# Attention row maxima: turned on TensorE and copied by two engines, or turned on VectorE and carried by DMA

## The reference

```
x = x + conv(ln(x)); t = x + ffn(ln(x))          # x: 4 images x 1024 tokens x 192
q, k, v = heads(x @ W + b)                       # 12 heads of 16
attn = q k^T / 4 + bias_h + bias_w               # 1024 x 1024 for each image and head
out  = softmax(attn) @ v ; conv = out @ Wp + bp
```

## Time and profile before

| | before |
|---|---|
| median of three runs | 905.75 us |
| profiled execution, its own time | 904.3 us |
| its span in the profile | 902.5 us |
| PE busy | 791.0 us, 88% of the span |
| DVE busy | 743.8 us, 82% |
| ACT busy | 558.8 us, 62% |
| POOL busy | 423.4 us, 47% |

### The profile page before, as it was taken

How to read it: one execution, slowest core, us unless ns; L and a number is a source line. 1 busy time by engine, 2 the same in 40 slices (tenths; PEclk the granted TensorE clock), 3 DMA queues, 4 the chain that set the end, 5 groups by cost and what they waited for, 6 DMA issues and landing times. The chain is left out here.

```text
span 902.5 us, 15297 instructions
## 1 busy us (share of the span) xinstructions
PE 791.0 (88%) x5848; PEld 407.7 (45%) x5848; DVE 743.8 (82%) x1493; ACT 558.8 (62%) x609; POOL 423.4 (47%) x263
## 2 busy tenths in 40 slices
PE   5899554479999999999999999999999999678874
PEld 2555454134444444444444444444444442256653
DVE  6998855498989988988998999998888894069995
ACT  1333345027777777777777777777777778447773
POOL 3777794436364454637263735445373324112220
PEclk9999788589999999999999999999999999889986
DMA  7676599999439392948567493939395000433411
GB/s 193 212 226 206 164 300 374 256 194 208 90 88 188 77 200 60 205 85 190 111 147 154 109 191 74 198 68 201 63 206 96 13 12 12 134 105 123 140 36 53
DMA packets 65675, 130.06 MB, mean 144 GB/s; under 512 B 9465, under 2 KB 45306, under 8 KB 57146
## 3 DMA queue, kind: packets, MB, share of 16 engines
q1 hardware_dynamic: 57634, 115.95, 56.2%
q10 hardware_dynamic: 7968, 13.13, 4.2%
HBM read 89.73 MB, written 34.60 MB: 138 GB/s over the span
## 5 line engine op out<-in xcount | busy, mean ns | idle before, releaser
L1065 DVE TENSOR_REDUCE at_piece_neg<-at_r_ps 128x1 f32<-128x512 f32 x768 | 482.8, 682 | 68.1 <-PE at_r_ps L935 64.7
L1028 ACT ACTIVATE at_probs<-at_s_ps 128x1024 f32<-128x1024 f32 x384 | 371.9, 1021 | 130.6 <-PE at_s_ps L956 129.3
L935 PE MATMUL at_r_ps<-op_mix_k,op_mix_q 128*128 128x256 f16 (+1 forms) x1920 | 282.0, 257 | 29.9 <-DMA op_mix_q<-bias_parts 17.8
L935 PEld LDWEIGHTS at_r_ps<-op_mix_k,op_mix_q 128*128 128x128 f16 x1920 | 148.2, 98 | 295.1 <-DVE at_piece_neg L1065 194.1
L850 POOL COPY op_mix_q<-op_mix_q 2x4096 f16<-2x4096 f16 x48 | 172.6, 3596 | 231.0 <-ACT op_mix_q L1033 230.5
L956 PE MATMUL at_s_ps<-op_mix_q,op_mix_k 128*128 128x512 f16 x768 | 227.7, 380 | 1.1 <-ACT at_probs L1028 0.5
L970 PE MATMUL at_o_ps<-at_probs,op_v_u 128*32 128x512 f32 x1536 | 204.2, 604 | 0.0
L218 POOL MEMSET op_mix_q<- 2x10240 f32 x12 | 103.5, 8627 | 0.6
L1033 ACT ACTIVATE op_mix_q<-at_r_ps 2x1024 f16<-2x1024 f16 x48 | 48.5, 1011 | 60.7 <-PE at_r_ps L946 60.7
L956 PEld LDWEIGHTS at_s_ps<-op_mix_q,op_mix_k 128*128 128x128 f16 x768 | 73.4, 98 | 19.6 <-ACT at_probs L1028 10.7
L854 POOL TENSOR_TENSOR at_o_sb<-at_o_sb,at_inv_rows 128x512 f32<-128x512 f32 x24 | 30.7, 1280 | 86.2 <-DVE at_inv_rows L1092 86.2
(11 more groups left out here) (121 smaller groups left out, 674.4 us busy)
## 6 DMA issues: line engine op xcount, KB each, us to landing
op_mix_q<-qk_parts SPq DMA_DIRECT2D x48, 640.0 KB, 10.7
op_mix_q<-bias_parts SPq DMA_DIRECT2D x120, 120.0 KB, 10.3
op_mix_q<-bias_parts SPq DMA_DIRECT2D x72, 128.0 KB, 10.3
bias_parts<-op_mix_q ACTq DMA_DIRECT2D x8, 1024.0 KB, 13.1
qk_parts<-op_mix_q SPq DMA_DIRECT2D x24, 256.0 KB, 2.3
v_rows<-pr_v_st SPq DMA_DIRECT2D x8, 768.0 KB, 4.1
op_mix_k<-qk_parts SPq DMA_DIRECT2D x48, 128.0 KB, 13.1
op_v_u<-v_rows SPq DMA_DIRECT2D x12, 512.0 KB, 14.2
```

The lines of the kernel that those rows point to most:

```text
L935: last = pe.matmul(r_bank("piece", at)[:, first % GROUP:first % GROUP + n], mix_q[owner.buf][:, variant, j, qt * P:(qt + 1) * P], mix_k[ow ...
L1028: act.activation(probs[n % PRING][:, 2 * pair:2 * pair + 2, :], s_ps[pair][:, :, :], ACT.Exp).then_inc(exp_done, 1)
L1065: dve.tensor_reduce(piece_neg[half][:, i:i + 1], r_bank("piece", at)[:, :], AX_X, ALU.max, negate=True).then_inc(reduced, 1)
```

## The change

Each half's 16 columns of maxima (four heads x four query tiles) are joined at once, with three operations of 16 columns in place of two times three of 8, at steps 4 and 12. DVE then turns the float16 tile of 128x32 (both parts side by side) in 32x32 blocks. ACT issues a transfer of the result to a small tensor in DRAM (128 runs of 64 bytes) at steps 5 and 13; POOL waits for it to land and issues five transfers from DRAM, one for each variant of the operand (two rows of four runs of 1 KB each). PE waits for the first of the five ahead of the first step of a half and for the other four ahead of the third. PE's transposes and the copies on ACT and POOL are gone, and with them two identity tiles and a third constant. The ring of three banks now runs on through all units. LEAD is 4, so four more pieces lie ahead of the first scores. On POOL, spread_max(unit, 1) moves from two places ahead of and behind zero_max to one ahead of it.

```diff
-    LEAD = 3
+    LEAD = 4
@@
-        for half in range(2):
-            for pair in range(2):
-                JOIN_AT[half, pair] = ((1 - half) * KT + (pair + 1) * (KT // 2) - LEAD) % STEPS
-                TURN_AT[half, pair] = JOIN_AT[half, pair] + 1
+        JOIN_AT = (2 * KT - LEAD, KT - LEAD)
+        ROWS_AT = (JOIN_AT[0] + 1, JOIN_AT[1] + 1)
@@
-        def r_bank(*use):
-            return r_ps[bank_of[use]]
+        def r_bank(unit, at):
+            return r_ps[(unit.u * PIECES + at) % RING]
@@ POOL
-                pool.tensor_copy(rows[:, 1:, :, :], rows[:, 0:1, :, :].to_broadcast([2, ops.VARIANTS - 1, 2, GROUP])).then_inc(max_spread, 1)
+                src = max_dram[half].rearrange("(h j t) p -> h j (t p)", h=2, j=QUAD)
+                pool.wait_ge(max_out[half], (unit.u + 1) * 16)
+                for variant in range(ops.VARIANTS):
+                    pool.dma_start(mix_q[unit.buf][MAX_ROW:MAX_ROW + 2, variant, :, half * GROUP:(half + 1) * GROUP],
+                                   src).then_inc((max_spread if variant else max_in)[half], 16)
@@ POOL, emit
-                spread_max(unit, 1, 0)
                 if not unit.first:
-                    pool.wait_ge(max_spread, unit.u * 4 + 3)
+                    pool.wait_ge(ops.max_zeroed, min(unit.u + 2, UNITS))
                     normalise(unit.after(-1), 1)
+                spread_max(unit, 1)
...
-                spread_max(unit, 1, 1)
-                if not unit.last:
-                    spread_max(unit.after(1), 0, 0)
...
                 normalise(unit, 0)
                 if not unit.last:
-                    pool.wait_ge(norm_done, unit.u * 2 + 1)
-                    spread_max(unit.after(1), 0, 1)
+                    spread_max(unit.after(1), 0)
@@ PE
-            def turn(unit, half, pair):
...
-                for t in range(2 * TILES):
-                    last = pe.transpose(max_rows(half * 2 + pair)[:, t * P:(t + 1) * P], neg_max[half][:, pair * 2 * TILES + t, :], ident16[:, :])
@@ PE, emit
+                    if n % KT == 0:
+                        pe.wait_ge(max_in[n // KT], (unit.u + 1) * 16)
                     if n % KT == 2:
-                        pe.wait_ge(max_spread, unit.u * 4 + (n // KT + 1) * 2)
+                        pe.wait_ge(max_spread[n // KT], (unit.u + 1) * (16 * (ops.VARIANTS - 1)))
@@ ACT
-            def row_max_in(unit, half, pair):
...
+            def max_to_rows(unit, half):
+                count = unit.u * 2 + half + 1
+                act.wait_ge(max_turned, count)
+                need(act, max_in[half], unit.u * 16)
+                need(act, max_spread[half], unit.u * (16 * (ops.VARIANTS - 1)))
+                act.dma_start(max_dram[half].rearrange("c (b r) -> b c r", r=SLOT), max_cols[half][:, :]).then_inc(max_out[half], 16)
@@ DVE, join_max
+                dve.tensor_tensor(row_neg[half][:, :], halves[:, :, 0], halves[:, :, 1], ALU.min).then_inc(row_joined, 1)
+                dve.tensor_tensor(neg_max[half][:, 0, :], halves[:, :, 0], halves[:, :, 1], ALU.min).then_inc(neg_hi, 1)
+                dve.wait_ge(row_joined, count)
                 dve.wait_ge(neg_hi, count)
+                dve.tensor_tensor(neg_max[half][:, 1, :], row_neg[half][:, :], neg_max[half][:, 0, :], ALU.subtract).then_inc(neg_done, 1)
+                dve.wait_ge(neg_done, count)
+                dve.transpose(max_cols[half][:, :], neg_max[half][:, :, :].rearrange("p h r -> p (h r)")).then_inc(max_turned, 1)
```

More of the change, by code:

```diff
@@ L792, in phase_attention @@
         BEFORE, AFTER = (0, 1, 1, 2, 2), 3
[L796 to L818, removed]
@@ L820, in phase_attention @@
-        assign(1)
-        assign(0)
-        def r_bank(*use):
-            return r_ps[bank_of[use]]
[L826 to L835, removed]
@@ L858, in _ @@
             ops.zero_max(pool, 1)
-            for pair in range(2):
-                spread_max(Unit(0, 0, 0), 0, pair)
+            spread_max(Unit(0, 0, 0), 0)
             def emit(unit):
-                spread_max(unit, 1, 0)
                 if not unit.first:
-                    pool.wait_ge(max_spread, unit.u * 4 + 3)
+                    pool.wait_ge(ops.max_zeroed, min(unit.u + 2, UNITS))
                     normalise(unit.after(-1), 1)
+                spread_max(unit, 1)
+                if not unit.first:
                     pool.wait_ge(norm_done, unit.u * 2)
@@ L931, in piece @@
                 qt = i // (PIECES // 2) * TILES + i // 2 % TILES
-                wait_bank(pe, unit, "piece", at)
+                need(pe, reduced, unit.u * PIECES + at - RING + 1)
                 for variant, first, n in ops.SEGMENTS:
                     if first // GROUP == kh:
-                        last = pe.matmul(r_bank("piece", at)[:, first % GROUP:first % GROUP + n],
+                        last = pe.matmul(r_bank(unit, at)[:, first % GROUP:first % GROUP + n],
                                          mix_q[owner.buf][:, variant, j, qt * P:(qt + 1) * P],
@@ L938, in piece @@
                 last.then_inc(piece_done, 1)
-            def turn(unit, half, pair):
-                owner = unit if half == 1 else unit.after(1)
-                pe.wait_ge(neg_done, (owner.u * 2 + half) * 2 + pair + 1)
-                wait_bank(pe, unit, "maxima", half * 2 + pair)
-                for t in range(2 * TILES):
-                    last = pe.transpose(max_rows(half * 2 + pair)[:, t * P:(t + 1) * P], neg_max[half][:, pair * 2 * TILES + t, :], ident16[:, :])
-                last.then_inc(max_rowed, 1)
             def scores(unit, n, j):
@@ L978, in _ @@
             for n in range(STEPS):
-                for half, pair in turned_at(n):
-                    if half == 0:
-                        turn(BEFORE_FIRST, 0, pair)
                 for at in pieces(n):
@@ L996, in emit @@
                         pe.wait_ge(ops.max_zeroed, nxt.u + 1)
-                    for half, pair in turned_at(n):
-                        if half == 1 or not unit.last:
-                            turn(unit, half, pair)
                     for j in range(QUAD):
@@ L1043, in emit @@
                 for n in range(STEPS):
-                    for half, pair in turned_at(n):
-                        if half == 1 or not unit.last:
-                            row_max_in(unit, half, pair)
+                    if n == ROWS_AT[1]:
+                        max_to_rows(unit, 1)
+                    if n == ROWS_AT[0] and not unit.last:
+                        max_to_rows(unit.after(1), 0)
                     exps(unit, n)
@@ L1095, in step_pieces @@
             def step_pieces(unit, n):
-                for half, pair in joined_at(n):
-                    if half == 1 or not unit.last:
-                        join_max(unit, half, pair)
+                if n == JOIN_AT[1]:
+                    join_max(unit, 1)
+                if n == JOIN_AT[0] and not unit.last:
+                    join_max(unit.after(1), 0)
                 for at in pieces(n):
```

78 lines of the change are left out of this document (26 added, 52 removed).

## The result

The changed kernel takes 972.83 us, the median of four runs (967.70 to 983.58), where the kernel before takes 905.87 beside it: a ratio of 1.0718 (95% interval 1.0665 to 1.0772), in which the longest run, a slow one 1.6% above the fastest, is left out. The profiled execution is that run, 983.58 with a span of 981.8, so I split its own difference of 79.3 us from the profiled execution of before and don't carry it over to the median.

The account below looks back on a forecast made before the run. It took PE to bound attention, DVE close behind. A gain of 18 us from 905.75 and 12 late row arrivals of 4.0 us, 48 in all, gave 935.7, say 936; range 883 to 965 at 8 in 10.

Parts of the forecast that it names:

- Turns, restart, stalls on PE: PE, per unit: turns gone, -2.60; bank restart at step 0 gone, -0.31; stalls behind invert 2.10 in place of 0.79, +1.31.
- The unit of 47.54 without late rows: Attention unit if row transfers arrive in time: 49.14 us less a net gain of 1.6.
- I take 0.23, as the tile is small: 0.60 a join: DVE's join at steps 3 and 11: extra wait and 128x32 transpose add 0.23 to the old 0.37 us.
- My fourth rival: Rows arrive, but the transpose costs 0.63 and more, each join 1.2, giving back 14 of 18 us: 902; chance 0.05.
- 8 x 0.63 = 5 us: ACT's row transfer beside loads: 8 runs an engine, each waiting for one load packet of 0.63 us, landing at 7.
- 0.35 + 2.0 + 4 x 0.63 = 4.9: POOL's first row transfer beside loads: 4 runs a row, each waiting for a load packet; 4.9 us in all.
- the case in which the rows are in time: First rival: row transfers pass the loads in one or two turns and arrive in time; 887.7 us, chance 0.30.
- The other four have 5.7 more: in time: Half 1's remaining four variants, behind the first at 8 of 9.5 us, have 5.7 us more and arrive in time.
- Half 0 late, 4.0 us, 12 times: Likeliest case: PE waits 4.0 us at ten unit starts and the first unit's two halves, 48 us; 936, chance 0.55.
- the third rival: Both halves late, by POOL's transfers on few engines or held ACT issue, and the clock falls; 966 us, chance 0.10.
- The first unit's two halves: Rows of both halves of the first unit late by 4.0 us each, as loads run on from the unit ahead.
- POOL loses its copies and issues ten transfers a unit: POOL in attention: zero_max queues some microseconds later behind ACT's transfer, but PE needs it only a unit on.

Follow-up runs that it names:

- the ring run: The kernel before with one edit: its three banks dealt on through all units instead of restarting at bank 0 each unit; 901.91 us, ratio 0.9943.
- LEAD 5: The changed kernel with LEAD 5 in place of 4, which puts the join a step ahead of invert; 984.59 us, ratio 1.0876.
- normalise held back: The changed kernel with POOL's normalise made to wait until the join's subtraction beside it is done; 980.55 us, ratio 1.0822.
- second profile of the same kernel: The changed kernel run again, unaltered, for another profile; 977.06 us.
- LEAD 5, light loads: The changed kernel at LEAD 5, loads from unit 3 on moving a sixteenth of the columns, every transfer still issued; 918.24 us, ratio 1.0137.
- the loads held: The changed kernel with SP's loads held until a half's rows have landed in all variants, unit 1's bias loads too; 941.76 us, ratio 1.0392.

## Why the prediction was wrong in size and place

I forecast 936 with a range to 965; the kernel takes 972.83. The direction and the mechanism (rows that wait behind loads) were right; the price of a row transfer, the place of the lateness and several other terms were not.

- **Turns, restart, stalls on PE: right.** Turn steps are plain; the restart was 0.31 a unit, shown alone by the ring run; the stall behind invert, predicted at 1.05 a half, is 1.01 at LEAD 5 and 1.00 with normalise held back. The unit of 47.54 without late rows was measured as 47.50.
- **"I take 0.23, as the tile is small: 0.60 a join": right for the transpose (0.21), wrong for the place.** Directly behind invert the join also meets POOL's normalise, which invert releases, and its subtraction takes 1.21 in place of 0.18. Steps 4 and 12 have 4.1 us a unit over plain steps, not 2.1; over 22 such steps that is 22 us. I had looked at what is queued behind the join on DVE, and not at what POOL runs at that moment. My fourth rival had a join of 1.2, for another reason.
- **"8 x 0.63 = 5 us" and "0.35 + 2.0 + 4 x 0.63 = 4.9", the price of a row transfer behind loads: the step that failed.** I counted a transfer's own packets, each waiting for one of a load. Behind the first packet that is about right (in unit 4, 160 of the rows and 170 of the loads). What the sum lacks is the wait ahead of the first packet: about ten load packets an engine, whatever the transfer's own size, 5.8 to 7.1 us with 8 KB and 3.1 to 3.5 with 4 KB. In unit 4 POOL's first transfer landed 9.6 us after its issue, 4.7 more than my 4.9. (A row of it is one packet of 4 KB in the trace, and not four, so that term had no ground either.) The queues' counts over 12 us can't show such a wait, as both queues had work all the time. The Trainium skill, page DMA: Bandwidth & Descriptors, section Queues, rings and completion order, says that an engine drains a whole packet of some 9 to 17 descriptors from one ring before it switches. I cited it as the case in which the rows are in time. The ten ahead of the first agree with that figure; the one for one behind it doesn't. Whether the ten are one turn of the loads' ring, or what an engine holds already when the transfer is issued, no run here shows.
- **"The other four have 5.7 more: in time", and half 1 as the safe half: wrong.** ACT's write for half 1 did pass ahead of the loads, as predicted (2.3 us to POOL's first issue). POOL's first transfer then took 9.6 us to land, not 4.9. Each transfer of a chain can meet such a wait: in half 1 the second did, in half 0 the first, in the first unit both.
- **"Half 0 late, 4.0 us, 12 times": seldom in this kernel, and right where nothing hides it.** Step 15 and step 0 hold 5.9 us in all here. The 2.0 lost at each subtraction and the wait at step 7 move half 0's write toward the end of the loads, and POOL's transfers find the engines free. Take those delays away (normalise held back, or LEAD 5), and half 0 is late in nine units: step 15 is 5.5 us over a plain one on average with normalise held back, and 6.2 at LEAD 5. That is why neither of these edits gained anything alone.
- **The clock: left out of the forecast.** The rows showed 0.50 for 3.41 us behind an idle time of 4.27, and I put it in the third rival only. In this kernel 15 of the 28 idle times of 1.5 us and more in units 0 to 10 are followed by it; behind the stalls that delay a step by 1.0 us (LEAD 5, light loads) it never came. Fourteen of the 15 lie at steps 5, 8 and 13 and are their 20 us, 1.4 each.
- **"The first unit's two halves" at 4.0 each: wrong.** The write waits 8.9 us behind unit 1's loads (issued at 190.34, first packet at 199.23), POOL's transfers wait 6.9 again, and PE idles 21.0 us at once. With the loads held, the first exponentials come at 201.6.
- **"POOL loses its copies and issues ten transfers a unit", costed at its issues alone: a term was missing.** It is the 7.3 us at the end of the phase.

In the profiled execution the terms are then: 22.4 first unit; 45 + 22 + 20 over plain steps in units 0 to 10, less the 39.1 that the kernel before has there; -0.9; 9.2. Sum 78.6 of 79.3, the rest being the other steps. By the second profile of the same kernel 1.9 of the 9.2 belong to that execution alone.

## What to carry to other kernels

A small transfer issued beside large ones waited here for about ten packets an engine of the other queue before its first one passed: 6 to 7 us with packets of 8 KB, and each transfer of a chain can meet it. Smaller packets of the bulk load, or holding it back for the small one, were worth more than an earlier issue. Once the rows were in time (LEAD 6, loads in three parts, row transfers issued by SP) the change went from 7% slower to 2% faster. And when an operation moves, look at all engines at its new place: a 16-column subtraction beside a POOL operation cost seven times its length, and one lateness hid another, so that mending one alone showed nothing.

## What the runs showed of the hardware

- A subtraction of two SBUF operands on DVE, 0.17 to 0.18 us alone, took 1.21 when a POOL operation on 128x512 had begun 0.09 us earlier.
- ACT's write of 128 runs of 64 bytes had its first packet 1.17 us after issue when the engines were free and its last 0.3 us later; at LEAD 5 behind loads of 8 KB packets the first came after 6.4 to 8.7 us, behind 4 KB packets after 3.3 to 4.3.
- Ahead of the first packet of POOL's half 1 transfers 158 to 177 load packets of 8 KB passed on the 16 engines, or 164 to 195 of 4 KB. Behind it the two queues passed about one for one where the loads had 8 KB packets (160 and 170 in unit 4).
- POOL issued a transfer in 0.55 us, and its first packet came 1.17 us after the issue when the engines were free. Where POOL had issued the 120 row transfers, its queue took 10.13 us at the phase's end; where it had issued none, 2.52 to 2.80.
- The granted clock went to half for 3.4 us behind 15 of 28 PE idle times of 1.5 us and more; in the run with light loads at LEAD 5 it stayed whole for 380 us with stalls of 1.0 us a half, in idle times of PE of 0.2 us at most.
